# Talking heads on Trainium2: the thresholds of the last 16 rows by a sorting network instead of by searches for the eight largest

## What is computed

```python
dots = jnp.einsum('bhid,bhjd->bhij', q, k) * QK_SCALE          # q, k normed; j = 4 memory keys + 128
dots = jnp.einsum('hg,bgij->bhij', W_pre_th, dots)
causal = jnp.arange(n)[:, None] < col_pos[None, :]              # col_pos = arange(j) - 4
dots = jnp.where(causal[None, None], mask_value, dots)
top = jax.lax.top_k(dots, TOPK)[0]                              # TOPK = 64
vk = top[..., -1:]                                              # the 64th largest of the row
dots = jnp.where(dots < vk, mask_value, dots)
attn = jax.nn.softmax(dots, axis=-1)
attn = jnp.einsum('hg,bgij->bhij', W_post_th, attn)
out = jnp.einsum('bhij,bhjd->bhid', attn, v)
```

## Time and profile before

| | us |
|---|---|
| median of 3 runs | 1331.24 (1329.02 to 1333.81) |
| the profiled execution's own time | 1336.64 |
| its span, first to last instruction | 1334.8 |
| DVE busy in the span | 971.2 (73%) |
| PE busy | 902.6 (68%) |
| ACT busy | 636.2 (48%) |
| POOL busy | 241.3 (18%) |

### The profile page before, as it was taken

The page is one execution under the profiler, slowest core; times in us unless marked ns, Lnnn a source line. Parts: engine busy times, 40 slices in busy tenths (PEclk is TensorE's granted clock), DMA queues, the critical chain, the costliest instruction groups (busy, mean ns, idle before and its releaser), DMA issues. The chain is left out here.

```text
span 1334.8 us, 18469 instructions
## 1 busy us (share of the span) xinstructions
PE 902.6 (68%) x6150; PEld 590.7 (44%) x6150; DVE 971.2 (73%) x2494; ACT 636.2 (48%) x1392; POOL 241.3 (18%) x370
## 2 busy tenths in 40 slices
PE   5964666745788402345797957898978626998876
PEld 3532233332455202234695633576645304566644
DVE  5859898956666399987455856798868497898822
ACT  4746777750444412353413731787437411666632
POOL 1320000001000000000012211189522022232100
PEclk9975555556899755676898987899979766999968
DMA  5000000001254300110100000000000000000000
GB/s 208 1 1 0 0 1 0 0 0 61 79 124 102 88 0 22 45 65 33 32 2 1 2 1 1 0 1 1 1 1 1 1 0 0 1 2 2 1 1 16
DMA packets 26607, 30.12 MB, mean 23 GB/s; under 512 B 1169, under 2 KB 23057, under 8 KB 25490
## 3 DMA queue, kind: packets, MB, share of 16 engines
q1 hardware_dynamic: 26514, 28.95, 7.7%
HBM read 19.50 MB, written 9.44 MB: 22 GB/s over the span
## 5 line engine op out<-in xcount | busy, mean ns | idle before, releaser
L1771 PEld LDWEIGHTS l2a_b_ps<-l2a_diag,l2a_uT 128*128 128x128 f32 x512 | 64.7, 194 | 29.1 <-issue 16.6
L1771 PE MATMUL l2a_b_ps<-l2a_diag,l2a_uT 128*128 128x128 f32 x512 | 69.2, 279 | 6.4 <-DVE l2a_convh L1982 5.4
L2468 PE MATMUL l1w_mem_ps<-l1a_rows,l1w_post 128*128 128x64 f32 x16 | 4.7, 391 | 95.7 <-DVE l1a_rows L2610 95.7
L2583 DVE MATCH_REPLACE8 l1w_minus<-l1w_low,l1w_minus 128x129 f32<-128x129 f32 (+39 forms) x264 | 64.4, 256 | 0.0
L2496 ACT ACTIVATE l1w_score<-l1w_mix_ps 128x264 f32<-128x264 f32 (+7 forms) x29 | 12.0, 451 | 108.9 <-DVE l1a_rows L2610 92.4
L2577 DVE MAX8 l1w_low<-l1w_minus 128x8 f32<-128x129 f32 (+37 forms) x332 | 59.5, 254 | 0.4
L2458 PE MATMUL l1w_mix_ps<-l1a_rows,l1w_pre 128*128 128x264 f32 (+7 forms) x58 | 30.5, 697 | 43.0 <-DMA l1a_rows<-scores_dram 24.8
L2441 POOL TENSOR_SCALAR_AFFINE_SELECT l1w_score<-l1w_score 128x256 f32<-128x256 f32 x8 | 4.1, 507 | 249.0 <-ACT l1w_score L2496 249.0
L2468 PEld LDWEIGHTS l1w_mem_ps<-l1a_rows,l1w_post 128*128 128x128 f32 x16 | 4.3, 306 | 100.7 <-DVE l1a_rows L2610 99.5
L583 ACT ACTIVATE l3a_l3x_probT<-l3a_l3x_turn_ps 128x512 f32<-128x512 f32 x64 | 38.2, 596 | 21.9 <-PE l3a_l3x_turn_ps L479 21.1
L1012 ACT ACTIVATE l0x_prob<-l0x_dist,l0x_last_mx 128x128 f32<-128x128 f32 x128 | 38.2, 386 | 21.5 <-DVE l0x_last_mx L1135 21.5
(11 more groups left out here) (579 smaller groups left out, 2809.9 us busy)
## 6 DMA issues: line engine op xcount, KB each, us to landing
scores_dram<-l1p_dots SPq DMA_DIRECT2D x8, 924.0 KB, 7.1
l1a_rows<-scores_dram SPq DMA_DIRECT2D x5, 1056.0 KB, 4.9
l1a_rows<-scores_dram SPq DMA_DIRECT2D x24, 132.0 KB, 3.6
scores_dram<-l1p_dots SPq DMA_DIRECT2D x8, 132.0 KB, 3.6
pack<-in_pack SPq DMA_DIRECT2D x1, 761.5 KB, 9.6
pack<-in_pack SPq DMA_DIRECT2D x2, 321.5 KB, 6.7
pack<-in_pack SPq DMA_DIRECT2D x1, 612.0 KB, 11.6
pack<-in_pack SPq DMA_DIRECT2D x1, 576.0 KB, 10.5
```

The costliest lines, as they stand in the source:

```text
L1771: mm = nc.tensor.matmul(bx_ps(n)[:, j * S:(j + 1) * S], uT[:, c, b, :], diag[:, s % 2, b, :], start=True, stop=True)
L2583: nc.vector.match_replace(out=neg[:, i, 0:keys[i]], in_to_replace=low[:, i, :], in_values=neg[:, i, 0:keys[i]], imm_value=LOWEST).then_inc ...
```

## The change

For the block of the last 16 rows (`SORTED = (7,)`) the rounds of MAX8 and MATCH_REPLACE are left out. Instead the 16 rows are treated in two halves of 8 rows. In each half, the first 128 of the 132 negated scores of each row are sorted in two groups of 64 by a bitonic network. A stage of the network (`exchange`) reads one buffer and writes the other: the lower of each pair with a minimum, the higher with a maximum. The two buffers are `minus`, whose rows stand 132 elements apart, and the new `swap`, whose 8 rows of 128 are contiguous. For each size 2, 4, ..., 64 the first exchange pairs an element with its mirror image in the group (a reversed view), and the others pair elements size/4, ..., 1 apart. A last minimum of one sorted group with the other reversed leaves the 64 smallest of the 128, and it writes them in front of the four keys left over. MAX8 over these 68 finds the threshold as their fifth largest (`at = MEM`).

Each exchange waits for both instructions of the one before. The next block's maximum is taken between the two halves. The other blocks keep their rounds, but `minus` has rows 132 apart for them too. To make room for `swap`, `pre` and `post` are computed in place in the pack, and `low` takes the place of `same_batch`, which is not read again.

```diff
+SORTED = (7,)
...
-        pre, post = sc.sb("pre", [128, 128]), sc.sb("post", [128, 128])
+        pre, post = cm.col("l1a_pre"), cm.col("l1a_post")
...
-        low = sc.sb("low", [128, ROWS_K, 8])
+        neg = minus[:].rearrange("p (i j) -> p i j", j=J)
+        swap = sc.sb("swap", [128, ROWS_K // 2, S])
+        low = cm.col("same_batch").rearrange("p (i e) -> p i e", e=8)
...
+                def exchange(low_out, high_out, a, b):
+                    after(dve, pair_set, pairs[0])
+                    nc.vector.tensor_tensor(low_out, a, b, ALU.min).then_inc(pair_set, 1)
+                    nc.vector.tensor_tensor(high_out, a, b, ALU.max).then_inc(pair_set, 1)
+                    pairs[0] += 2
+
+                def sort(rows, w):
+                    if w < J:
+                        nc.vector.memset(neg[:, rows, w:], -LOWEST).then_inc(pair_set, 1)
+                        pairs[0] += 1
+                    here, there = neg[:, rows, 0:S], swap[:]
+                    size = 2
+                    while size <= TOPK:
+                        groups = lambda z: z.rearrange("p r (g e) -> p r g e", e=size)
+                        lower = lambda z: groups(z)[:, :, :, 0:size // 2]
+                        mirror = lambda z: groups(z)[:, :, :, size // 2:][:, :, :, ::-1]
+                        exchange(lower(there), mirror(there), lower(here), mirror(here))
+                        here, there = there, here
+                        step = size // 4
+                        while step:
+                            near = lambda z: z.rearrange("p r (g e) -> p r g e", e=2 * step)[:, :, :, 0:step]
+                            far = lambda z: z.rearrange("p r (g e) -> p r g e", e=2 * step)[:, :, :, step:]
+                            exchange(near(there), far(there), near(here), far(here))
+                            here, there = there, here
+                            step //= 2
+                        size *= 2
+                    dve.wait_ge(pair_set, pairs[0])
+                    nc.vector.tensor_tensor(neg[:, rows, TOPK:S], here[:, :, 0:TOPK], here[:, :, TOPK:S][:, :, ::-1],
+                                            ALU.min).then_inc(pair_set, 1)
+                    pairs[0] += 1
+                    dve.wait_ge(pair_set, pairs[0])
...
-                        a = cut[0] * w
...
-                        nc.vector.tensor_scalar(minus[:, a:ROWS_K * w], score[n % 2][:, a:ROWS_K * w], -1.0, None,
+                        nc.vector.tensor_scalar(neg[:, cut[0]:, 0:w], s[:, cut[0]:, :], -1.0, None,
                                                 ALU.mult).then_inc(minus_set, 1)
...
-                        for r in range(max(keys[i] - TOPK for i in cut) // 8 + 1):
+                        by_sort = k in SORTED
+                        if by_sort:
+                            sort(slice(0, ROWS_K // 2), w)
+                            maximum(n + 1)
+                            sort(slice(ROWS_K // 2, ROWS_K), w)
+                            for i in cut:
+                                nc.vector.max(low[:, i, :], neg[:, i, TOPK:J]).then_inc(kth, 1)
+                                n_kth += 1
+
+                        for r in range(0 if by_sort else max(keys[i] - TOPK for i in cut) // 8 + 1):
...
-                            at = (keys[i] - TOPK) % 8
+                            at = MEM if by_sort else (keys[i] - TOPK) % 8
```

More of the change, by code:

```diff
@@ L2396, in mixed_weights @@
                  "exp_set", "minus_set", "kth", "taken", "bound_set", "kept", "recip_set", "weights_set", "at_mm", "at_set", "mem_mm",
[L2397 removed]
+                 "mem_set", "mem_stored", "pair_set")
         (pad_set, mats_set, mix_mm, mix_set, causal_set, max_set, neg_set, exp_set, minus_set, kth,
[L2399 removed]
+         taken, bound_set, kept, recip_set, weights_set, at_mm, at_set, mem_mm, mem_set, mem_stored, pair_set) = (sc.sem(n) for n in names)
         def block_of(buf, k):
@@ L2457, in mix @@
                         i = f * m
-                        nc.tensor.matmul(mix_ps[u % 4][:, 0:m * w], pre[:],
+                        nc.tensor.matmul(mix_ps[u % 4][:, 0:m * w], pre,
                                          blocks[n % ROW_BUFS][:, i:i + m, 0:w], start=True,
@@ L2467, in mix_again @@
                         pe.wait_ge(mem_set, n)
-                    nc.tensor.matmul(mem_ps[:, 0:MEM * ROWS_K], post[:], weights[:, :, 0:MEM].rearrange("p i m -> p m i"),
+                    nc.tensor.matmul(mem_ps[:, 0:MEM * ROWS_K], post, weights[:, :, 0:MEM].rearrange("p i m -> p m i"),
                                      start=True, stop=True).then_inc(mem_mm, 1)
@@ L2475, in mix_again @@
                             mm = nc.tensor.matmul(at_ps[u % 2][:, i, :], weights[:, 4 * f + i, MEM:],
-                                                  post[:], start=True, stop=True)
+                                                  post, start=True, stop=True)
                         mm.then_inc(at_mm, 1)
@@ L2534, in _ @@
                 cm.need(dve, "l1a")
-                nc.vector.scalar_tensor_tensor(out=pre[:], in0=cm.col("l1a_pre"), scalar=QK_SCALE,
+                nc.vector.scalar_tensor_tensor(out=pre, in0=cm.col("l1a_pre"), scalar=QK_SCALE,
                                                in1=cm.col("same_batch"), op0=ALU.mult, op1=ALU.mult).then_inc(mats_set, 1)
-                nc.vector.tensor_tensor(post[:], cm.col("l1a_post"), cm.col("same_batch"), ALU.mult) \
+                nc.vector.tensor_tensor(post, cm.col("l1a_post"), cm.col("same_batch"), ALU.mult) \
                     .then_inc(mats_set, 2)
```

4 lines of the change are left out of this document (1 added, 3 removed).

## The result

The changed kernel takes **1337.76 us** (median of 4 runs, 1337.26 to 1338.06) against 1332.22 for the kernel before in the same comparison (4 runs). The ratio is 1.0044, with a 95% interval of 1.0028 to 1.0061. It is slower, by 5.5 us, and the forecast was 1336.8. The profiled execution took 1338.02 us around a span of 1336.2.

What follows compares the result with a forecast made beforehand. The prediction took the first block's threshold search on DVE to bound the kernel. Removing 54.1 us and adding 59.7 us gives 5.6 us more, so 1331.24 + 5.6 = 1336.8 us, range 1332 to 1350.

Steps and rivals of the forecast that it cites:

- What bounds the kernel: First block's threshold search on DVE: other engines wait for its end, so each microsecond there is one in the span.
- What goes: First block's search: 130 MAX8 and 114 MATCH_REPLACE removed, 54.12 us without the next block's maximum.
- What comes: First block's sort: 42 exchanges 56.0 us, two final minimums 1.45, 16 MAX8 2.3; sum 59.7 us.
- The lower bound: Sort priced from L273's 0.659 us per 512-element instruction: total 56.8 us, 2.7 us more than the removed search.
- Access patterns: Exchange operands in the sort: gaps, backwards reading and every-other-element access all costed at nothing.
- rival (a): Single-word accesses in 24 sort instructions cost 12.8 us, 18.4 more in all, 1349.6; chance 0.20.
- the 11.4 us: Extra cost of the 24 single-word sort instructions by the skill's stream rule, giving 1348; not taken into the forecast.
- Rival (c): Sort's minimums and maximums stream two per cycle; kernel 17.3 us faster, 1313.9; chance 0.06 together with others.
- Edits costed at nothing: Constants in the pack, negation into rows 132 apart, later next-block maximum and POOL contention: 0 us.
- The chances: Odds for the whole kernel's time: forecast 0.62; slower 0.74, same 0.20, faster 0.06.
- Rival (b): Sort's exchanges come at the lower bound, 2.7 us more, 1333.9, no measurable change; chance 0.12.

Runs made afterwards that it cites:

- mixed search: First block with 13 rows sorted by the network at once and three rows searched by MAX8 and replacements between exchanges; ratio to the kernel before 1.0008.
- sixteen rows: Changed kernel with all 16 rows in one sort, 21 exchanges of 1024 elements, next block's maximum after it; ratio to the kernel before 0.9995.
- layout probes: Changed kernel plus 32 unread minimums of 512 elements in eight layouts; one trace: step of two free, three costs 0.16 us, four 0.38 us.
- places alone: Changed kernel with the sort switched off (SORTED = ()), keeping the moved storage and the negation into rows 132 apart; ratio to the kernel before 1.000.
- interleaved sort: Changed kernel with the two halves' exchanges issued in turn, each waiting only for the exchange before the last; ratio to the kernel before 1.0006.

## Why the prediction was right

- *What bounds the kernel.* Right: the first block's end came 5.64 us later in its stretch, and 5.5 us appeared in the median. The sentence that a microsecond more or less in the search is one in the span holds for more, within 3 us for one block and 6 us for two. For less it was too simple: 3.6 us fewer in the block gave nothing that can be measured (8.1 fewer gave 5.9, with an interval of 3.3 to 8.5 that leaves one for one open).
- *What goes.* 54.12 us, the same rows as in the earlier trace rows; the mixed search and the sixteen rows are consistent with it.
- *What comes.* 59.7 us predicted, 59.75 found, of which 0.26 are the one slow exchange named below, which the sum didn't have; the other terms, each a little smaller than predicted, cancel it. The terms: an exchange 1.333 predicted, (519.53 - 491.63) / 21 = 1.329 found; 16 searches in 68 elements 2.3, found 2.22 (520.26 to 522.48). The block's +5.6 is the sum's +5.6. The lower bound, L273's 0.659, was never reached: L2561 took 0.685 to 0.695.
- *Access patterns.* Right, and this was the largest risk. All 84 instructions, in every layout, stand at 0.69 but one:

```profile
L2561 DVE TENSOR_TENSOR l1w_swap<-l1w_minus x22: 685/693/695, 462.1 to 518.2; 128x512 f32<-128x512 f32 x22
L2562 DVE TENSOR_TENSOR l1w_swap<-l1w_minus x22: 683/685/953, 462.7 to 518.8; 128x512 f32<-128x512 f32 x22
...
L2561 DVE TENSOR_TENSOR l1w_minus<-l1w_swap x20: 691/692/694, 463.5 to 516.9; 128x512 f32<-128x512 f32 x20
L2562 DVE TENSOR_TENSOR l1w_minus<-l1w_swap x20: 682/685/687, 464.1 to 517.5; 128x512 f32<-128x512 f32 x20
```

  So rival (a) is out, and with it the 11.4 us that the prediction worked out from the Trainium skill's "Vector Engine (DVE) Microarchitecture Reference", "Measured stream behaviour on trn2"; the layout probes show how near it was, since the gap of one word is the last free step. Backwards reading is free as well. Rival (c) is out by the same rows.
- *Edits costed at nothing.* Storage, negation and later maximum: nothing, by the places alone and by sixteen rows. POOL's work "too little for any contention with it to matter" is the one term that was put at nothing and wasn't quite: the 953 ns above is an exchange instruction beside POOL's selection, 0.26 us more than its neighbours. It is that small because POOL reads SBUF once in the block; beside products an exchange more than doubles. In the interleaved sort POOL itself lost 18.4 us.
- *The chances.* The forecast's own range, 1334 to 1340, held. Rival (b), 1333.9, lies 3.9 us below the result, and below all its runs.

## What to carry to other kernels

Count the elements as well as the instructions: 102 instructions for 244 lost, because 84 of them carried 512 elements at 1.05 ns each (0.69 us for 512, 1.23 for 1024), and half the row count doubled the number of starts and dependent gaps. Price a chain as start-to-start for the independent step (0.61 us) and end plus 0.04 us for the dependent one (0.73), and put as many rows in an instruction as the buffer allows: from 8 rows to 16 the same sort went from 59.75 to 54.05 us. In this kernel a gain of 3.6 us in one stage didn't reach the time. Where a gain of that size is expected, look in the stages behind it as well before counting it.

## What the runs showed of the hardware that was not expected

- A DVE chain of two-tensor instructions, one every 0.60 us without a pause, kept a 0.51 us POOL instruction that reads SBUF waiting for 18.9 us. With a pause of 0.04 us after every second instruction it was through in 0.75 us, but between the two instructions of a pair and not in the pause, so the reason isn't known. POOL's memsets (0.52 us each) slowed no exchange (0.69).
- For 512 f32 elements: 0.69 us at a step of one or two words, 0.85 at three, 1.07 at four and 1.06 to 1.07 at a hop of 132, whether one operand hops or three.
- Kernels that differ in one block of 60 us alone had mean granted clocks from 0.783 to 0.788, and in the runs of one kernel a thousandth goes with 0.88 us.
